# Routing steps, quarter moves and the order of the opening stage of a fused scan and expert kernel

## What is computed

```python
xn = _layernorm(x)                                   # x: 4 x 512 x 512
# recurrence, per batch and feature
projected = einsum('bsd,ed->bse', xn, W_in)
state = d * state + (1.0 - d) * seg_t                # d = sigmoid(decay), over s
attn = einsum('bsd,ed->bse', stacked, W_out) + bias
# experts: 32 of them, six per token, capacity 768
scores = softmax(x2d @ wg_router.T); topk_w, topk_idx = top_k(scores, 6)
ye = einsum('ecf,efd->ecd', silu(xe @ w_gate) * (xe @ w_up), w_down)
y  = sum(ye of the token's experts * topk_w)
sh = (silu(x2d @ ws_gate) * (x2d @ ws_up)) @ ws_down
out = x + attn + y + sh
```

## Time and profile before

| | us |
|---|---|
| median of 3 runs (931.1 to 939.1) | 933.65 |
| profiled execution | 935.56 |
| its span in the profile | 933.7 |
| PE busy | 910.3 |
| DVE busy | 644.4 |
| ACT busy | 520.7 |
| POOL busy | 389.4 |

### The profile page before, as it was taken

The page is one execution under the profiler, slowest core; times in us unless marked ns, Lnnn a source line. Parts: engine busy times, 40 slices in busy tenths (PEclk is TensorE's granted clock), DMA queues, the critical chain, the costliest instruction groups (busy, mean ns, idle before and its releaser), DMA issues.

```text
span 933.7 us, 13995 instructions
## 1 busy us (share of the span) xinstructions
PE 910.3 (97%) x4480; PEld 808.2 (87%) x4480; DVE 644.4 (69%) x1140; ACT 520.7 (56%) x877; POOL 389.4 (42%) x318
## 2 busy tenths in 40 slices
PE   7899999999998999999999999999999999999997
PEld 6768877888887899999999999999999899998885
DVE  6868858656446777677777667766767667658665
ACT  7984541212134665666665666766666567557561
POOL 3001000010301556666767665666457546555321
PEclk9999999999999999999999999999999999999999
DMA  8352254222544999989899899899999999999855
GB/s 332 138 192 102 89 194 139 90 60 94 173 126 118 300 250 237 242 237 259 219 232 230 232 235 264 235 231 233 281 245 233 255 259 247 243 246 275 194 111 124
DMA packets 127723, 191.30 MB, mean 205 GB/s; under 512 B 16384, under 2 KB 73488, under 8 KB 127392
## 3 DMA queue, kind: packets, MB, share of 16 engines
q1 hardware_dynamic: 102480, 132.56, 45.2%
q0 software_dynamic: 23856, 57.29, 29.7%
q10 hardware_dynamic: 1312, 0.53, 0.2%
HBM read 121.16 MB, written 42.61 MB: 175 GB/s over the span
## 4 chain that ended last, share of the span: by engine, by line
PE 58%; DMA 10%; SPq 8%; DVE 7%; issue 6%; ACT 5%; POOL 4%; POOLq 1%; ACTq 1%; DVEq 0%
PE p_gu L1256 11%; PE p_gu L1258 11%; PE p_gu L1257 11%; SPq L520 8%; DMA xnT<-xn_rows,ids 6%; PE p_y L1256 6%; PE p_y L1257 6%; PE p_y L1258 6%; DMA xnT<-xnT 2%; POOL xnT L769 2%; POOL out L783 2%; DVE w_lo L1573 2%; DMA xnT<-xn_rows 1%; ACT w_hi L859 1%; PE p_gu L1378 1%
## 5 line engine op out<-in xcount | busy, mean ns | idle before, releaser
L783 POOL DMA_INDIRECT out<-rows,ids x112 | 200.9, 1794 | 218.2 <-ACT rows L859 193.9
L1256 PE MATMUL p_gu<-xT_hi,w_hi 128*128 128x512 f32 (+12 forms) x816 | 287.5, 352 | 2.9 <-DVE xT_lo L1573 2.9
L1258 PE MATMUL p_gu<-xT_hi,w_lo 128*128 128x512 f32 (+12 forms) x816 | 287.2, 352 | 0.0
L1257 PE MATMUL p_gu<-xT_lo,w_hi 128*128 128x512 f32 (+12 forms) x816 | 287.1, 352 | 0.0
L769 POOL DMA_INDIRECT xnT<-xn_rows,ids x112 | 163.2, 1457 | 110.1 <-DVE xT_lo L1573 45.3
L1573 DVE TENSOR_TENSOR w_lo<-raw,w_hi 128x1024 fp32r<-128x1024 f32 (+2 forms) x148 | 173.7, 1178 | 9.6 <-ACT w_hi L859 9.6
L1256 PEld LDWEIGHTS p_gu<-xT_hi,w_hi 128*128 128x128 f32 x816 | 153.7, 188 | 14.9 <-DVE xT_lo L1573 3.3
L1257 PEld LDWEIGHTS p_gu<-xT_lo,w_hi 128*128 128x128 f32 x816 | 153.8, 189 | 11.5
L1258 PEld LDWEIGHTS p_gu<-xT_hi,w_lo 128*128 128x128 f32 x816 | 153.6, 188 | 7.9
L859 ACT ACTIVATE w_hi<-raw 128x1024 fp32r<-128x1024 f32 (+2 forms) x148 | 151.3, 1027 | 2.8 <-PE p_gu L1258 2.1
L1256 PE MATMUL p_y<-w_hi,hT_hi 128*128 128x512 f32 (+1 forms) x368 | 145.1, 394 | 4.9 <-ACT rows L859 2.2
(11 more groups left out here) (227 smaller groups left out, 1050.8 us busy)
## 6 DMA issues: line engine op xcount, KB each, us to landing
raw<-L_ffn_w_gate SPq DMA_DIRECT2D x32, 704.0 KB, 5.6
raw<-L_ffn_w_up SPq DMA_DIRECT2D x32, 704.0 KB, 7.9
xnT<-xnT SPq DMA_DIRECT2D x424, 48.0 KB
raw<-L_ffn_w_down SPq DMA_DIRECT2D x32, 512.0 KB, 8.5
raw<-L_ffn_w_down SPq DMA_DIRECT2D x32, 192.0 KB, 9.5
xring<-out SPq DMA_DIRECT2D x20, 256.0 KB, 3.5
out<-xring SPq DMA_DIRECT2D x20, 256.0 KB, 2.4
xnT<-xnT SPq DMA_DIRECT2D x80, 64.0 KB
```

The costliest lines, as they stand in the source:

```text
L783: pool.indirect_dma_start(out=out[:, :], in_=y_sb[t][0:n, :], in_offset=None, out_offset=bass.IndirectOffsetOnAxis(ap=ids[0:n, col:col + 1 ...
L1256: t_.matmul(dst, stat[0], mov[0], start=first, stop=False)
L1257: t_.matmul(dst, stat[0], mov[1], start=False, stop=False)
L1258: return t_.matmul(dst, stat[1], mov[0], start=False, stop=last)
```

## The change

Three things are changed. The order of calls in the opening is different on ACT and DVE, and chunk 0 of every batch's first projection is now done in the order that only batch 0 had. The routing steps are moved: `st_lo(3)` comes ahead of `constants` and `load_order`, `shift(3)` goes into unit 0, `main_slots` from unit 0 to 1, `extra_slots` from unit 0 to 3, and shifts 4 to 6 and one `extra_experts` one unit later. And SP issues all sixteen quarter moves of the first routed unit.

```diff
@@ SP @@
-            quarters(sp, SH, range(QUARTERS // 2))
+            quarters(sp, SH)
             quarters(sp, SH + 1)
@@ ACT @@
             xb_hi(0)
+            reorder(0)
             deviation(4)
-            reorder(0)
-            reorder(1)
             normalise(4)
             normalise(5)
+            deviation(6)
+            normalise(6)
+            q(0, 0)
+            normalise(7)
+            q(0, 1)
+            reorder(1)
+            deviation(8)
             wT_hi(1, 0)
             wT_hi(1, 1)
-            wT_hi(1, 2)
-            deviation(6)
-            wT_hi(1, 3)
-            normalise(6)
-            normalise(7)
-            q(0, 0)
-            q(0, 1)
-            deviation(8)
-            reorder(2)
-            st_hi(0, [0])
-            reorder(3)
             normalise(8)
             q(0, 2)
-            st_hi(0, [1])
             normalise(9)
+            xb_hi(1)
             q(0, 3)
-            st_hi(0, [2])
-            xb_hi(1)
+            st_hi(0, [0])
+            reorder(2)
+            wT_hi(1, 2)
+            wT_hi(1, 3)
+            reorder(3)
+            st_hi(0, [1, 2])
             reorder(4)
             reorder(5)
             q(1, 0)
...
-                    quarters(act, SH, range(QUARTERS // 2, QUARTERS))
@@ PE @@
-            def in_proj_first():
+            def in_proj_high_first(b):
-                w, x = w_inT, xb_of(0)
+                w, x = w_inT, xb_of(b)
                 for c in range(DC):
                     pe.wait_ge(s_wth, c + 1)
-                    pe.wait_ge(s_xbh, c + 1)
+                    pe.wait_ge(s_xbh, DC * b + c + 1)
...
+                    if m == 0:
+                        in_proj_high_first(b)
+                        continue
                     for c in range(DC):
-                        if m == 0 and b > 0:
-                            pe.wait_ge(s_xb, DC * b + c + 1)
@@ DVE @@
             w_lo_T(0, 3)
+            xb_lo(0)
             measure(4)
-            xb_lo(0)
             factors(4)
             measure(6)
+            factors(6)
             tile_evac(4)
-            factors(6)
-            w_lo_T(1, 0)
             tile_evac(5)
-            measure(8)
             scan_of(0, 0)
-            scan_of(0, 1)
-            factors(8)
-            st_lo(0, [0])
             tile_evac(6)
             tile_evac(7)
+            scan_of(0, 1)
+            measure(8)
+            factors(8)
+            w_lo_T(1, 0)
+            w_lo_T(1, 1)
+            st_lo(0, [0])
             scan_of(0, 2)
+            xb_lo(1)
+            scan_of(0, 3)
             st_lo(0, [1])
             tile_evac(8)
             tile_evac(9)
-            xb_lo(1)
             measure(10)
             measure(12)
             factors(10)
             factors(12)
-            scan_of(0, 3)
             st_lo(0, [2])
-            w_lo_T(1, 1)
             w_lo_T(1, 2)
...
+            st_lo(3)
             constants()
             load_order()
-            st_lo(3)
-            shift(3)
...
-                0: (expert_order, main_slots, extra_slots, lambda: shift(4)),
-                1: (lambda: shift(5), lambda: shift(6)),
-                2: (lambda: shift(7), lambda: shift(8), segments),
-                3: (main_rows, extra_rows, lambda: extra_experts(0), lambda: extra_experts(TILES)),
+                0: (expert_order, lambda: shift(3)),
+                1: (main_slots, lambda: shift(4), lambda: shift(5)),
+                2: (lambda: shift(6), lambda: shift(7), lambda: shift(8), segments),
+                3: (extra_slots, main_rows, extra_rows, lambda: extra_experts(0)),
```

More of the change, by code:

```diff
@@ L1282, in in_proj_first @@
                 for c in range(DC):
-                    pe.wait_ge(s_xb, c + 1)
+                    pe.wait_ge(s_xb, DC * b + c + 1)
                     mm = t_.matmul(p_gu[0][:], w[0][:, c, 0:P], x[1][:, c, :], start=False,
@@ L1327, in _ @@
             keep_running(10)
-            in_proj_first()
-            in_proj(0, [1])
+            in_proj(0, [0, 1])
             tile_T(4)
@@ L2017, in _ @@
             routing = {
-                0: (expert_order, main_slots, extra_slots, lambda: shift(4)),
-                1: (lambda: shift(5), lambda: shift(6)),
-                2: (lambda: shift(7), lambda: shift(8), segments),
-                3: (main_rows, extra_rows, lambda: extra_experts(0), lambda: extra_experts(TILES)),
-                4: (lambda: extra_experts(2 * TILES), lambda: extra_experts(3 * TILES), extra_blocks),
+                0: (expert_order, lambda: shift(3)),
+                1: (main_slots, lambda: shift(4), lambda: shift(5)),
+                2: (lambda: shift(6), lambda: shift(7), lambda: shift(8), segments),
+                3: (extra_slots, main_rows, extra_rows, lambda: extra_experts(0)),
+                4: (lambda: extra_experts(TILES), lambda: extra_experts(2 * TILES), lambda: extra_experts(3 * TILES), extra_blocks),
             }
```

## The result

The changed kernel takes 941.26 us (median of 6 runs, 937.57 to 941.95), the kernel before, on the same chip, 932.78 us (median of 6, 931.1 to 939.1). The ratio is 1.0073, with a 95% interval from 1.0046 to 1.01: slower by 6.8 us (4.3 to 9.3, as shares of 932.78), and within the 1% of the forecast. The two medians themselves are 8.5 us apart (0.9%); the ratio weighs all the executions. Forecast for the median was 939.3, in a range of 929.5 to 943.5. Each ratio in this document is of executions in the faster of two states; one of run 2's twelve took 1005.87 us at a granted clock of 0.85 and is not in its ratio. The profiled execution of the changed kernel took 941.18 us with a span of 939.4 us; before it was 935.56 and 933.7. So profile stands against profile with +5.62 us, where the sum had said +5.6. That fit is closer than the steps behind it, as will be seen.

What follows compares the result with a forecast made beforehand. It took PE, busy for 910.3 us with few waits, as the bound. Opening +3.8 and +0.4, routing steps -2.2 and quarter moves +3.6 summed to +5.6 us: 939.3 us on the median, 0.6% slower, range 929.5 to 943.5.

Steps and rivals of the forecast that it cites:

- DVE's stand: Opening: DVE idles 4.7 us, to 35.9, for ACT's first states' high part; batch 1's last chunk starts 4.3 us late.
- The opening, first gains: First projection: earlier low parts bring PE to chunk 1 at 18.4 and chunk 2 at 25.3, a gain of 1.3 us.
- Rival A: Opening: DVE does not stand, so the opening gains 2.1 us; total -0.7, 933.0 us; chance 0.14.
- The low clock of the opening: Opening: old low-clock spell left as it is; another behind 46 us could cost up to 1.7, taken as 0.4 us.
- The opening in sum: Whole opening: a loss of 3.8 us from the orders, and 0.4 us more for low clock.
- The routing steps: Ahead of and in unit 0: PE's waits of 0.6 and 1.6 us go, nothing else is late; -2.2 us.
- The quarter moves: First routed unit: sixteen SP issues at 0.64 us land 3.6 us later; PE's wait 6.5 instead of 2.92; +3.6 us.
- My upper bound: Quarter moves at the first routed unit: 0.75 us an issue, which would cost +5.3 us.
- The clock behind that wait: Behind PE's wait for the first routed unit: no low-clock cost in the sum; 1.7 us more in rival D.
- rival D: Opening and routed unit: longer waits bring more low clock, issues cost 0.75 us; total +9.9, 943.5 us; chance 0.15.
- Rival B: Quarter moves: the issue does not set their landing, so they cost nothing; total +2.0, 935.7 us; chance 0.13.
- Rival C: Rival A and rival B together, the faster side: total -4.3, 929.3 us; chance 0.06.

Runs made afterwards that it cites:

- run 2: The kernel before with only the opening's new orders on PE, ACT and DVE: 940.05 us, ratio 1.0053.
- run 1: The kernel before with only the quarter moves changed, all sixteen of the first routed unit on SP: 937.82 us, ratio 1.0038.
- run 3: The kernel before with only the moved routing steps: 930.02 us, ratio 0.9944.
- run 8: Run 7's kernel with a reworked opening, ACT's q and `xb_hi` ahead of reorders: 935.5 us, ratio 1.0005 to the kernel before.
- run 9: Run 8's kernel with shared weights' loads behind four row stores, not eight, and the logits' copy ahead of the last four reorders: 925.46 us, 0.9915 to the kernel before.
- run 7: The kernel before with run 6's early quarter moves and run 3's routing steps, old opening: 926.75 us, ratio 0.9907.
- run 4: The changed kernel with DVE's `st_lo(0, [0])` moved behind `xb_lo(1)` and the fourth scan: 938.93 us, ratio 1.0045 to the kernel before.
- run 10: The changed kernel with quarter moves again eight on SP and eight on ACT: 935.3 us, ratio 1.004 to the kernel before.
- run 6: The kernel before with all sixteen quarter moves on SP, issued earlier, ahead of four tiles' stores and loads: 928.64 us, ratio 0.9934.
- run 5: The kernel before with the quarter moves split twelve on SP and four on ACT: 936.77 us, ratio 1.002.

## Why the prediction was right, and where its steps were off

The time, the sign and the size were as forecast: +5.6 predicted, +5.62 from profile to profile, +6.8 (4.3 to 9.3) by the ratio. All three parts had the sign given to them, shown by runs 1, 2 and 3 each by itself. The mechanisms that the sum rests on, DVE's stand, the two waits behind routing steps and the row of issues, were all seen. But several terms were off and cancelled, and that the two profiles agree with the sum to 0.02 us is luck.

**The opening, first gains: the size off.** Chunk 1 was to start at 18.4 and chunk 2 at 25.3; they started at 19.40 and 26.10, so 0.5 us was gained of 1.3. The granted clock at 10 to 14 us was 0.69 where it was full in the profile before, and PE began the projection at 16.20. In runs 8 and 9, with the same calls up to there and a full clock in that window, chunk 1 started at 18.11 and 18.21. So the step's arithmetic held, and what it had not reckoned with was another execution's clock.

**DVE's stand: right.** 4.7 us to 35.9 were predicted, 4.39 us to 36.4 measured, released by ACT's high part. Rival A is out. `xb_lo(1)` ended at 40.66 (40.2), and batch 1's last chunk started at 50.35 (50.0), released by q, as written. Chunk 0 of batch 1 was over at 41.3 (40.4): 0.46 of that is DVE's, and some of the rest is PE's clock, which had just fallen. In run 2, at full clock, PE was over 0.40 behind the last low part, here 0.65.

**The low clock of the opening: another spell, little cost.** I left the spell at 27 to 31 as it was. It was gone after (clock 1.0), and one of 8 us at 0.55 to 0.60 came at 38 to 46. It stood ahead of a chunk that waited for ACT's q anyway, so it cost almost nothing: in run 2 the clock in those windows was full and the last chunk came at 50.55 all the same. So the 0.4 of my sum stands for nothing that a run shows.

**The opening in sum:** +4.1 against 4.2, and this agreement is partly luck. The profile before had a full clock at 10 to 14 us and the one after had not. Runs 3 and 7 have the old opening with the low clock there, and their shift at 119.6 is already +3.09 and +2.85; against them the new opening is only 1.0 to 1.5 us late. No trace of the change's own opening has the full clock there, so how the 4.1 parts into order and clock is open (the last section has the rows). That the new order costs something is shown by the timed runs (run 2). Run 4 showed what the prediction had not said: with 4.4 us of DVE's lateness taken from `xb_lo(1)`, three quarters of the last chunk's lateness stay, behind ACT's order.

**The routing steps: -2.85 instead of -2.2.** Both waits went. Where the list of waits had 0.6 and 1.6, the shift fell by 0.95 (119.6 to 135.9) and by 1.9 (135.9 to 161). In every pair with this part the fall was the same: 2.85 in the change, in run 3 and in run 10 (4.22 to 1.38). I had cut my count at the waits that the list names; the 0.6 us beyond them were not traced further. By the times of run 3 (-5.2, -7.2 to -3.4) this would be the term that was mis-sized most; runs 7 and 10 don't bear out so large a gain.

**The quarter moves: the term that was mis-sized most in the traces.** The mechanism was right (sixteen issues in a row on SP, DVE waiting on the last landing). The step took 0.64 an issue from SP's own seven and came to 3.6. Measured were 0.71 an issue in the mean and a wait of 7.46 instead of 6.5, +4.54. The 0.64 was right for an issue in a steady row; what the sum lacked is a slow issue among the first, 1.51 us here and 1.62 in run 1. The early sixteen of run 6 had none over 0.80, and took 0.67 in the mean. My upper bound, 0.75 an issue, would have given +5.3; the value lay between the two.

**The clock behind that wait: counted at nothing, cost 1.25 us.** It was rival D's term, with 1.7. The low clock behind the wait lasted 5.4 us against 2.8. But this looks like the one execution's and not the change's: run 1, with the longer wait (7.60), had 3.3 us of it, and run 10, with the short one (3.20), about 5.8. Rival D's other half, more low clock in the opening, cost nothing at 38 to 46 us.

**The end: counted at nothing, gave back 1.35 us.** Nothing in the prediction spoke of it. Between 640 and 900 us, where the DMA engines are busy for 0.94 of the time and more, the shift fell by 0.9 here, by 2.7 in run 3, by 4.0 in run 10 and by 0.4 or less in runs 2 and 9. The change touches nothing there. So this looks like a difference from one execution to the next, and the fit to 0.02 us rests on it as much as on my terms. Without this and the low clock behind the wait, which nearly cancel, the same traces would have stood at +5.8.

**Rivals B and C** are out by run 1 and by run 5, in which the wait grew with the number of issues at the same bytes.

## What to carry to other kernels

When small transfers are moved onto one queue, price them at their issue time times the whole count, with some room for a slow one, and ask before any split whether they can be issued earlier: all sixteen on one queue, ahead of four tiles' stores, were 0.66% faster than the split over two engines, and the same sixteen behind those stores 0.38% slower. When a hand-written order is changed, follow both engines' lists past the first stall, as the next limit is often right behind it (run 4) or in the queue that frees a buffer (run 8). And compare several executions before reading a gain of 3 us out of two traces: the same order reached its logits up to 4 us apart here.

## What the runs showed of the hardware

**The opening isn't the same in each execution.** PE's logits started, with the old order, at 62.1 in runs 1, 5 and 6, at 63.2 in the profile before, and at 66.1 to 66.3 in runs 3 and 7, whose opening is word for word the same. The two late ones had a granted clock of 0.60 at 10 to 14 us and 0.69 to 0.70 at 22 to 26, where the others had 1.0. The profiles of the new opening (the change, runs 2, 4 and 10) all had 0.64 to 0.69 at 10 to 14, and their logits at 67.4 to 67.6 (66.2 in run 4). The same window in the kernel before, in run 3 and after the change (the clock is the third number from the end):

```profile
10.00:14.00 4.00, 3.06 (x26) 3.06 (x27) 3.28 (x7) 3.92 (x7) 0.00 (x0) 1.00 1.07 411
10.00:14.00 4.00, 3.14 (x15) 3.15 (x16) 2.11 (x4) 3.59 (x6) 0.00 (x0) 0.60 1.07 408
10.00:14.00 4.00, 3.06 (x16) 3.06 (x17) 2.43 (x5) 3.60 (x6) 0.00 (x0) 0.69 1.08 415
```

The old and the new order are the same up to there, and runs 8 and 9, which begin like the new one, had the full clock, so why it differs is open; and up to 3 of the 4.1 us between the two profiles' openings may be this. The profiled executions of runs 3 and 7, with the late start, are 2.6 and 3.0 us slower than the medians of their runs, while those of the change and run 2 are at theirs. So the timed ratio of run 2, 0.53% or 4.9 us (2.9 to 6.9), doesn't depend on one execution's clock. How often a timed execution of either order has the low clock there was not recorded, so its part in the 4.9 isn't known.

**At one place, a longer wait did not bring a longer low clock.** Behind the wait for the first routed unit PE ran at 1.2 GHz for about 2.8 us in the profile before (wait of 2.92) and 5.4 after (7.46), which looks like a rule. Runs 1 and 10 break it. These are their stretches at 290 to 300 us, run 1 with PE's first matmul at 290.32 behind 7.60 of waiting, run 10 with it at 288.57 behind 3.20:

```profile
290.00:300.00 10.00, 9.68 (x39) 8.56 (x40) 4.36 (x9) 4.41 (x9) 4.54 (x6) 0.82 0.60 148
290.00:300.00 10.00, 10.00 (x40) 8.78 (x39) 4.16 (x7) 3.70 (x6) 3.82 (x6) 0.78 0.53 143
```

A mean of 0.82 over 10 us is 3.6 us at the lower level, 3.3 of them behind the first matmul; 0.78 is 4.4, and with the stretch from 288.57 to 290 about 5.8. In run 6, where PE didn't wait, the clock was full.

**An issue of these small moves costs 0.60 us and a gap of 0.04, with a slow one now and then:** 0.64 in the mean of the seven before, and for each from the fifth on after. The mean of fifteen is 0.71 because of slow issues among the first four, one of them of 1.51 us; ACT's eight had one of 1.41. What makes them slow wasn't tried.
